# One list for all banks of mixed terms, and weighing turns of 28, 28, 28 and 30 matmuls

## What is computed

```python
def _cin_forward(x, Ws):          # Ws = (W0 of 39 x 39 x 128, W1 of 39 x 128 x 128)
    x0 = x
    h = x
    outs = []
    for W in Ws:
        h = jnp.einsum('bid,bjd,ijh->bhd', x0, h, W)
        outs.append(h)
    out = jnp.concatenate(outs, axis=1)
    return out.sum(axis=-1)
```

## Time and profile before

| | us |
|---|---|
| median of 3 runs | 250.3 (250.0 to 250.98) |
| the profiled execution, its own time | 250.63 |
| its span, first to last instruction | 248.8 |
| PE busy with matmuls | 238.8 (96%) |
| PE loading weights (beside matmuls) | 203.0 (82%) |
| DVE busy | 178.0 (72%) |
| ACT busy | 167.8 (67%) |
| matmul instructions on L494 | 1194 |
| matmul instructions on L537 | 1680 |

### The profile page before, as it was taken

How to read it: one execution, slowest core, us unless ns; L and a number is a source line. 1 busy time by engine, 2 the same in 40 slices (tenths; PEclk the granted TensorE clock), 3 DMA queues, 4 the chain that set the end, 5 groups by cost and what they waited for, 6 DMA issues and landing times.

```text
span 248.8 us, 12083 instructions
## 1 busy us (share of the span) xinstructions
PE 238.8 (96%) x5578; PEld 203.0 (82%) x5578; DVE 178.0 (72%) x318; ACT 167.8 (67%) x309; POOL 0.6 (0%) x8
## 2 busy tenths in 40 slices
PE   1999999999999989999999999999999999999994
PEld 0577799968888878888888888888888888888993
DVE  1056999999958799699799779969969967700000
ACT  2489980042615458888887888888887888888300
POOL 0000000000000000000000000000000000000000
PEclk9999999999999999999999999999999999999999
DMA  5999100110101202522432252152252240110111
GB/s 177 418 396 403 69 0 7 16 22 36 57 3 54 56 9 26 167 56 25 137 104 18 41 190 30 30 171 59 26 149 86 25 114 22 16 25 18 11 25 30
DMA packets 15523, 20.66 MB, mean 83 GB/s; under 512 B 9424, under 2 KB 10352, under 8 KB 15088
## 3 DMA queue, kind: packets, MB, share of 16 engines
q1 hardware_dynamic: 15472, 19.89, 28.2%
HBM read 17.35 MB, written 0.52 MB: 72 GB/s over the span
## 4 chain that ended last, share of the span: by engine, by line
PE 77%; DVE 13%; SPq 4%; DMA 2%; ACT 2%; issue 1%; DVEq 0%
PE psum L537 34%; PE psum L518 22%; PE psum L494 12%; PE psum L477 7%; SPq L310 4%; PE psum L550 3%; DVE arena L377 3%; DVE arena L358 2%; DVE arena L361 2%; ACT arena L451 2%; DMA arena<-in_w 1%; DVE arena L398 1%; DVE arena L382 1%; DVE arena L402 1%; DMA arena<-arena 1%
## 5 line engine op out<-in xcount | busy, mean ns | idle before, releaser
L451 ACT COPY arena<-psum 64x460 f32<-64x460 f32 x256 | 137.6, 538 | 54.7 <-PE psum L518 51.7
L537 PEld LDWEIGHTS psum<-arena 128*64 128x64 f32 x1680 | 93.4, 137 | 10.5 <-issue 10.3
L537 PE MATMUL psum<-arena 128*64 128x128 f32 x1680 | 100.4, 274 | 0.0
L518 PE MATMUL psum<-arena 64*32 64x230 f32 x2048 | 57.4, 357 | 1.2 <-DVE arena L402 1.2
L358 DVE TENSOR_TENSOR arena<-arena 128x1600 f32<-128x1600 f32 x32 | 58.2, 1820 | 0.0
L361 DVE TENSOR_TENSOR arena<-arena 128x1520 f32<-128x1520 f32 x32 | 55.6, 1736 | 0.0
L494 PE MATMUL psum<-arena 128*32 128x128 f32 (+3 forms) x1194 | 48.9, 318 | 0.0
L494 PEld LDWEIGHTS psum<-arena 128*32 128x32 f32 x1194 | 43.2, 109 | 6.0 <-issue 2.3
L518 PEld LDWEIGHTS psum<-arena 64*32 64x32 f32 x2048 | 37.8, 106 | 12.5 <-issue 4.4
L477 PE MATMUL psum<-arena 128*32 128x230 f32 x512 | 27.9, 385 | 5.4 <-DMA arena<-in_w 5.4
L431 ACT COPY arena<-psum 64x460 f32<-64x460 f32 x44 | 25.9, 589 | 8.6 <-PE psum L477 8.0
(11 more groups left out here) (11 smaller groups left out, 11.2 us busy)
## 6 DMA issues: line engine op xcount, KB each, us to landing
arena<-in_x SPq DMA_DIRECT2D x32, 312.0 KB, 3.8
arena<-in_v_first SPq DMA_DIRECT2D x1, 1520.0 KB, 7.7
arena<-in_v_second SPq DMA_DIRECT2D x1, 1520.0 KB, 11.3
arena<-in_w SPq DMA_DIRECT2D x1, 1280.0 KB, 7.2
arena<-in_w_ones SPq DMA_DIRECT2D x2, 448.0 KB, 11.0
arena<-in_w SPq DMA_DIRECT2D x2, 320.0 KB, 3.5
arena<-in_w SPq DMA_DIRECT2D x1, 640.0 KB, 4.6
arena<-arena SPq DMA_DIRECT2D x24, 26.2 KB
```

The lines of the kernel that those rows point to most:

```text
L451: done = nc.scalar.copy(view(s0[n % 2] + EXTRAS * q * B + 8 * in_batch + 4 * odd, (B, SLOTS), (2, 2), (1, 2), rows=(HALF * q, HALF * q + H ...
L518: done = nc.tensor.matmul(bank_view((COUPLES[couple(g)] + r) * BANK + m, (2, LIST), rows=(ROWS * c, ROWS * c + ROWS)), view(x0 + u % X_RIN ...
L537: nc.tensor.matmul(bank_view(at + HID, (1, HID), rows=(HALF * side, HALF * side + HALF)), view(s0[n % 2] + j * B, (1, B)), view(c0 + j * H ...
```

## The change

`mixed_order` takes the place of `mixed_steps`. The calls of each quarter are the same, in the same order and with the same widths; they are now put into one list over all 29 banks. The quarter with the fewest columns so far gets the next call, among those quarters whose next call lies in the bank of the quarter furthest behind or in the one after. PE waits for a bank's place ahead of the first call of that bank in this list, and `mixed_filled` is raised by the last one. The sums stand behind the last call of banks 10, 15, 20 and 25 as before. As quarters, one digit a call, the lists begin:

```diff
-def mixed_steps(slots, pair_of):
-    waiting = []
-    for quarter in range(4):
-        of = [terms(quarter % 2, pair_of[quarter][j]) for j in slots]
-        steps = []
...
+def mixed_order(pair_of):
+    turns = range(-(-SLOTS // IN_BANK))
+    waiting = [[] for _ in range(4)]
+    for quarter, steps in enumerate(waiting):
+        for k in turns:
+            slots = range(IN_BANK * k, min(IN_BANK * k + IN_BANK, SLOTS))
+            of = [terms(quarter % 2, pair_of[quarter][j]) for j in slots]
+            first = len(steps)
...
     columns, order = [0] * 4, []
     while any(waiting):
-        quarter = min((q for q in range(4) if waiting[q]), key=lambda q: columns[q])
-        _, row, j, m, count = waiting[quarter].pop(0)
-        order.append((quarter, row, j, m, count))
+        behind = min(steps[0][0] for steps in waiting if steps)
+        quarter = min((q for q in range(4) if waiting[q] and waiting[q][0][0] <= behind + 1), key=lambda q: columns[q])
+        k, row, j, m, count = waiting[quarter].pop(0)
+        order.append((k, quarter, row, j, m, count))
         columns[quarter] += count
     return order
...
-                each = -(-(SLOTS - EXTRAS) // BATCH_UNITS)
+                each = 28
...
-            for k in range(MIXED):
-                mixed(k)
-                if k in SUMS_BEHIND:
-                    sums(2 * SUMS_BEHIND[k])
-                    sums(2 * SUMS_BEHIND[k] + 1)
+            order = mixed_order(PAIR_OF)
+            last_step = {step[0]: i for i, step in enumerate(order)}
+            banks_begun, quarters_begun = set(), set()
+            for i, (k, c, row, j, m, count) in enumerate(order):
+                if k not in banks_begun:
+                    mixed_bank_free(k)
+                    banks_begun.add(k)
+                done = nc.tensor.matmul(
...
+                    start=(k, c) not in quarters_begun, stop=True, skip_group_check=True)
+                quarters_begun.add((k, c))
+                if i == last_step[k]:
+                    done.then_inc(mixed_filled, 1)
+                    if k in SUMS_BEHIND:
+                        sums(2 * SUMS_BEHIND[k])
+                        sums(2 * SUMS_BEHIND[k] + 1)
```

More of the change, by code:

```diff
@@ L82 @@
 V_ROWS = len(v_tables())
-def mixed_steps(slots, pair_of):
-    waiting = []
-    for quarter in range(4):
-        of = [terms(quarter % 2, pair_of[quarter][j]) for j in slots]
-        steps = []
[L94 to L104, removed]
+IN_BANK = 4
+def mixed_order(pair_of):
[6 more added lines that the diff above has]
+            first = len(steps)
+            for t in range(2):
+                for j, some in zip(slots, of):
+                    if t >= len(some):
+                        continue
+                    row, m = some[t]
+                    last = steps[-1] if len(steps) > first else None
+                    if last and last[1] == row and last[2] + last[4] == j and last[3] + last[4] == m:
+                        last[4] += 1
+                    else:
+                        steps.append([k, row, j, m, 1])
+            assert len(steps) > first
     columns, order = [0] * 4, []
     while any(waiting):
-        quarter = min((q for q in range(4) if waiting[q]), key=lambda q: columns[q])
-        _, row, j, m, count = waiting[quarter].pop(0)
-        order.append((quarter, row, j, m, count))
+        behind = min(steps[0][0] for steps in waiting if steps)
+        quarter = min((q for q in range(4) if waiting[q] and waiting[q][0][0] <= behind + 1), key=lambda q: columns[q])
+        k, row, j, m, count = waiting[quarter].pop(0)
+        order.append((k, quarter, row, j, m, count))
         columns[quarter] += count
@@ L150, in cin_kernel @@
     W1_LOADS = [(0, 1), (1, 2), (2, 4), (4, 8)]
-    IN_BANK = BANK // HID
+    assert IN_BANK == BANK // HID
     MIXED = (SLOTS + IN_BANK - 1) // IN_BANK
@@ L482, in _, with mixed_bank_free @@
                 done.then_inc(direct_filled, 1)
-            def mixed(k):
-                bank = mixed_bank(k)
+            def mixed_bank_free(k):
                 if k < 8:
@@ L490, in mixed @@
                     pe.wait_ge(c_added, k - 8 + 1 if k < 12 else k - 4 + 1)
[L491 to L500, removed]
             def sums(g):
@@ L556, in _ @@
             pe.wait_ge(v_ready, 1)
-            for k in range(MIXED):
-                mixed(k)
-                if k in SUMS_BEHIND:
-                    sums(2 * SUMS_BEHIND[k])
-                    sums(2 * SUMS_BEHIND[k] + 1)
+            order = mixed_order(PAIR_OF)
[6 more added lines that the diff above has]
+                done = nc.tensor.matmul(
+                    bank_view(mixed_bank(k) * BANK + j % IN_BANK * HID, (1, count * HID), rows=(ROWS * c, ROWS * c + ROWS)),
+                    view(v0 + row * ROWS, (1, ROWS)),
+                    view(w1_0 + m * PIECE, (PIECE, count), (PLACES * PIECE, PIECES), (1, PIECE)),
+                    start=(k, c) not in quarters_begun, stop=True, skip_group_check=True)
[5 more added lines that the diff above has]
+                        sums(2 * SUMS_BEHIND[k] + 1)
             for u in range(BATCH_UNITS, UNITS):
```

## The result

The changed kernel takes **271.0 us** (median of 4 runs, 270.76 to 271.8) against 250.56 for the kernel before in the same session (4 runs, 250.0 to 250.98): a ratio of 1.0823, 95% interval 1.0789 to 1.0857. It is 20.4 us slower; 273.5 was forecast, range 268.5 to 277.

A forecast was written before the change was run, and what follows sets the result against it. The prediction took PE's matmuls to bound the kernel; 22.8 us for the mixed order plus 0.36 for the weighing made 23.2, on the 250.3 median 273.5 us, range 268.5 to 277.

The forecast's parts named there:

- What bounds the kernel: Whole kernel: PE busy 96% of the span, its matmuls end to end from 54.25 us on; DVE has slack.
- How PE hands work to the strips: Mixed stage: PE hands out instructions in program order, holding three unstarted per strip; the next for that strip blocks everything behind.
- The mixed order: Mixed stage: the new list makes 26 runs of three to eight strip 1 calls, blocking other strips; +22.8 us.
- The marks set for this step: Mixed stage profile: five-bank stretches about 13.3 us, last 6.6; loads per us down over a third; ACT's copies wait longer.
- The guards' price of 0: Mixed stage: bank guards stand about one bank earlier, yet waits for DVE adds cost 0, with 4 us to spare.
- The weighing: Weighing: three calls move to earlier turns at 0.1185 us each; only the last batch's sums lack cover, +0.36 us.
- the mark set for this step: Weighing, steady part of the changed profile: turns of 5.04 us three times and one of 5.2.
- The sum: Whole kernel: 22.8 + 0.36 = 23.2 us added to the median of 250.3, giving 273.5 us.
- deep queues: Rival, strips' queues: at least 16 instructions held, so only the weighing's cost remains, 250.7 us; chance 0.07.
- Two or four held: Rivals, strip queues: two held, +30.6, 281 us (dearer-run rival, 0.05); four held, +17.3, 268 (more-than-three rival, 0.05).
- a bank that is reported late: Part of the dearer-run rival, mixed stage: filled banks reported late because order of completion binds; rival's chance 0.05.
- The faster rival: Mixed stage: borders between banks are the loss; deep queues plus balanced columns recover it, 248.7 us; chance 0.03.

The follow-up runs named there:

- the order alone: The changed kernel with the old weighing turns (27, 27, 27 and 24 + 9 calls): 273.32 us against 250.11 for the kernel before.
- the turns of 28 alone: The kernel before, old lists per bank kept, with weighing turns of 28, 28, 28 and 21 + 9 calls: 247.74 us against 250.11.
- without the runs: The change's list with a shut-out strip counted on so it has nothing to catch up, old weighing: 250.98 us against 250.09.

## Why the prediction was right, and where not

**What bounds the kernel**: right. The loss is PE's own busy time; no wait of PE's matmuls for another engine grew by more than 0.34 us (the one for ACT's last copies, below). One reading of the chain was too wide: it is PE's work only up to the last sums, at 227.8 us in the kernel before; behind them ACT's last copies, the issue of SP's 13 gathers (L310, 3.7% of the span) and the last landing stand in it.

**How PE hands work to the strips**: right, and the step on which all hung. Two tails of the old stage gave the three held instructions; the runs of two and three calls, 254.34 and 292.43 us for 254.9 and 292, show it with nothing changed but the order within the banks.

**The mixed order**: right within 3%. Banks 0 to 10: 26.15 us (32.26 to 58.41) for 25.8; the first sums 1.72 for 1.71; five banks 13.34 for 13.26; the last three 6.59 for 6.6. With the order alone the kernel was 23.2 us slower, 22.8 had been the sum. The marks set for this step appeared too: 210 loads in 13.30 us against 208 in 8.40, over a third fewer in a us, and ACT's copies waited 55.7 us during the stage against 34.2. The guards' price of 0 held too: in the changed kernel PE waits for no DVE add from the start of the stage to its last bank, and the wait that shows without the runs, 0.58 us, is one that the sum had called covered.

**The weighing**: this step failed, in sign and size: +0.36 forecast, about -2.4 us measured in the changed kernel, and -2.4 with the turns of 28 alone (247.74 against 250.11). The prediction divided 3.20 us by 27 calls and moved three calls at 0.1185. The price hangs on the longer side: 28 calls cost what 27 do, so the first three turns stayed as long and the sums did not come later; the fourth fell by two places of 0.22 us. Six batches give 2.6 us, since the last fourth turn stands behind the last sums, where ACT's copies now keep PE's matmuls waiting 0.34 us. A second row of the kernel before's chain would have shown it, the fourth turn with its 24 calls:

```profile
106.53 2.77 PE psum L537 x48
```

(3.20 - 2.77) / 3 is 0.143, not 0.1185; a price per call that differs between two lengths is no price per call. It is 2 x 0.215 for two places of the longer side, 14 against 12. Of the mark set for this step, turns of 5.04 us three times and one of 5.2, the three did not appear: in the chain of the changed kernel the sums of a batch begin at 132.57, 137.50, 142.42 and 147.34 us, the next at 152.49, 4.92 to 4.93 apart three times, as before, and then 5.15.

**The sum**: 273.5 for 271.0. On the profiled executions it is 273.8 for 270.8, 3.0 too much: 2.8 from the weighing's term (-2.4 in place of +0.36) and 0.9 from the earlier start of the stage, which nothing in the sum stood for, less the 0.7 by which the stage was longer than forecast. The time came out inside the range with the weighing's sign wrong because that term is small beside the stage's.

**The rivals**: deep queues are out (292 us with runs of three). The Trainium skill, "TensorE: Matmul & The Clock Gate", Part 3, "The mechanism", gives the PE a 64-deep reorder window. Taken as a depth for each strip, as the prediction tried it, that is out by the same run. Two or four held are out by the runs of two and of three; a bank that is reported late costs nothing that shows, since PE waits for no DVE add within the changed stage. The faster rival, a list over all banks that frees the strips from the banks' borders, was tried without the runs: 250.98, no gain.

**What remains open**: why the mixed stage begins between 31.9 and 33.3 us in kernels whose part ahead of it is the same; and whether three are held for each strip in tiles of other shapes, as in the sums (64 x 32) or the weighing (128 x 64), was not tried; nor was whether it is the matmul or its weight load that is held.

## What to carry to other kernels

Where matmuls of several column strips share PE, write the program so that the strips take turns call by call: in this kernel, with float32 calls of two instructions each, two calls of a strip in a row cost 4.2 us and three cost 42.3. Balance over a whole list doesn't help if it is reached in bursts, and a strip that was shut out must not catch up at once. PE's busy share says nothing on this: count the loads in short stretches, or divide a stretch by the blocks of its longest strip. And before a price per call is used, see whether calls go in pairs: read the same line at two lengths.

## What the runs showed of the hardware

With float32 tiles of 128 x 32, PE hands instructions out in the order of the program, and of those bound to one 32-row strip it holds three that have not started: what stands behind a run begins with the 13th of 16 instructions in the kernel before (34.45 and 36.20 us) and with the 7th of 10 in the changed one (76.28 us). Runs of four instructions cost 4.2 us in this kernel, runs of six 42.3 us. A strip that ran empty takes about 25 ns longer for its first matmul (617 ns against 592).
